# Attention with adaptive layer norm: key block 6 of the second query half goes from TensorE's sums product to GpSimd's running sums

## What is computed

```
mod = (silu(c) @ wmod).reshape(B, 6, 1, -1)            # sa, ca, ga, sb, cb, gb
h   = layernorm(x) * (1 + ca) + sa
q, k, v = h @ Wq, h @ Wk, h @ Wv                       # 32 query heads, 8 key heads, width 32; q, k rotated
att   = where(causal, q @ k.T / sqrt(32), -inf)        # four query heads share one key head
probs = softmax(att)
x = x + ga * ((probs @ v) @ Wo)
h = layernorm(x) * (1 + cb) + sb
x = x + gb * (h @ W.T + bias + lora(h))
```

## Time and profile before

| | |
|---|---|
| time, median of 3 runs (lowest to highest) | 2407.32 us (2406.97 to 2408.16) |
| profiled execution: its time | 2411.02 us |
| profiled execution: span, first to last instruction | 2409.2 us |
| busy over the span: PE / DVE / ACT / POOL | 2349.1 / 1764.7 / 1023.2 / 1577.9 us |
| GpSimd adds (L1101): number, busy | 434 (14 a group, groups 0 to 30), 921.1 us |

### The profile page before, as it was taken

How to read it: one execution, slowest core, us unless ns; L and a number is a source line. 1 busy time by engine, 2 the same in 40 slices (tenths; PEclk the granted TensorE clock), 3 DMA queues, 4 the chain that set the end, 5 groups by cost and what they waited for, 6 DMA issues and landing times. The chain is left out here.

```text
span 2409.2 us, 37318 instructions
## 1 busy us (share of the span) xinstructions
PE 2349.1 (98%) x13260; PEld 1647.3 (68%) x13260; DVE 1764.7 (73%) x4224; ACT 1023.2 (42%) x1868; POOL 1577.9 (65%) x834
## 2 busy tenths in 40 slices
PE   5999999999999999999999999998999999999998
PEld 3788888888655555555555555544788888888886
DVE  4766667667999999999999999975545545555553
ACT  3433333331466666666666666775111111111111
POOL 3743334341698998999989999984654654654653
PEclk8999999999999999999999999999999999999999
DMA  6523333334355336334343345404323333333330
GB/s 239 200 88 115 121 120 118 123 110 122 92 165 154 85 88 175 83 83 134 77 103 86 86 138 124 103 19 151 110 93 104 107 94 99 111 95 96 113 89 27
DMA packets 179716, 267.22 MB, mean 111 GB/s; under 512 B 20508, under 2 KB 113884, under 8 KB 178400
## 3 DMA queue, kind: packets, MB, share of 16 engines
q1 hardware_dynamic: 179552, 265.13, 37.3%
HBM read 183.22 MB, written 80.81 MB: 110 GB/s over the span
## 5 line engine op out<-in xcount | busy, mean ns | idle before, releaser
L1101 POOL TENSOR_TENSOR p_sum<-p_sum,p_ring 128x768 f32<-128x768 f32 (+1 forms) x434 | 919.4, 2154 | 67.9 <-PE ctx_ps L1162 44.6
L995 ACT ACTIVATE p_ring<-scores 128x512 f32<-128x512 f32 (+1 forms) x896 | 444.3, 575 | 299.4 <-DVE scores L1049 224.3
L290 DVE CUSTOM_DVE_ANT_0 scores_q<-scores_q,mask_row 128x512 f32<-128x512 f32 x977 | 458.6, 514 | 33.8 <-PE scores_q L277 33.5
L277 PE MATMUL scores_q<-k_stack,q_stack 96*128 96x512 f32 (+1 forms) x1473 | 437.7, 372 | 6.6 <-DVE neg_max L290 6.0
L277 PEld LDWEIGHTS scores_q<-k_stack,q_stack 96*128 96x128 f32 x1473 | 252.9, 190 | 211.0 <-DVE neg_max L294 96.9
L1141 PE MATMUL scores<-q_stack,k_stack 98*128 98x512 f32 (+1 forms) x1216 | 371.7, 395 | 1.7 <-DVE neg_max L290 0.9
L646 POOL TENSOR_TENSOR roped_hilo<-roped_hilo 128x512 fp32r<-128x512 f32 x80 | 105.3, 1316 | 337.2 <-ACT roped_hilo L489 337.2
L294 DVE TENSOR_REDUCE neg_max<-scores_q 128x1 f32<-128x512 f32 x496 | 313.0, 684 | 3.6 <-PE scores_q L277 1.5
L695 PE MATMUL proj_ps<-h_hi,w_hi 128*128 128x512 f32 x752 | 297.8, 396 | 0.7 <-POOL w_lo L635 0.7
L695 PE MATMUL proj_ps<-h_hi,w_lo 128*128 128x512 f32 x752 | 293.6, 390 | 0.0
L695 PE MATMUL proj_ps<-h_lo,w_hi 128*128 128x512 f32 x752 | 293.2, 390 | 0.0
(11 more groups left out here) (169 smaller groups left out, 3657.2 us busy)
## 6 DMA issues: line engine op xcount, KB each, us to landing
q_stack<-qk_t SPq DMA_DIRECT2D x96, 512.0 KB, 6.9
qk_t<-roped_hilo SPq DMA_DIRECT2D x80, 512.0 KB, 2.8
x_in<-in_L_attn_resid SPq DMA_DIRECT2D x32, 512.0 KB, 6.3
ctx_t<-ctx_raw SPq DMA_DIRECT2D x64, 256.0 KB, 7.5
prefetched<-in_L_wmod SPq DMA_DIRECT2D x4, 4096.0 KB, 14.7
prefetched<-ctx_t SPq DMA_DIRECT2D x31, 512.0 KB, 4.1
prefetched<-inv_t SPq DMA_DIRECT2D x124, 128.0 KB, 5.4
k_stack<-qk_t SPq DMA_DIRECT2D x96, 128.0 KB, 8.7
```

The lines of the kernel that those rows point to most:

```text
L277: last = nc.tensor.matmul(dst[:, a, :], qs[0:MHI, h, i * P:(i + 1) * P], ks[0:MHI, lo:lo + w], start=True, stop=True)
L290: last = nc.vector.tensor_tensor_reduce(src[:, a, :], src[:, a, :], sh.maskW[:, HALF - w:HALF], -1.0, LARGE, ALU.add, ALU.min, neg[:, a, :])
L995: nc.scalar.activation(p[:, a * per:(a + 1) * per, :], src[:, a * per:(a + 1) * per, :], ACT.Exp, scale=SM_SCALE).then_inc(s_ex.sem, 1)
L1101: nc.gpsimd.tensor_tensor(a, a, probs(n, u), ALU.add).then_inc(s_ap.sem, 1)
```

## The change

Key block 6 of half 1 (tick 18) leaves `TAIL`: GpSimd gets an add for it, and the sums product no longer takes it out of the ring. `NP` rises from 14 to 15 adds a group and `POOL_DONE[1]` with it. The hand-written order is laid anew: the sums product of half 1 of the group before moves from behind tick 5 to behind tick 13, the maxima are spread over the ticks otherwise, quads 5, 6 and 7 come together behind tick 15, and `INV_AT` is moved by four ticks.

```diff
-TAIL_FROM = {0: 4, 1: 6}
+TAIL_FROM = {0: 4, 1: 7}
...
-INV_AT = (9, 12, 15)
+INV_AT = (13, 16, 19)
...
 AFTER = [
     [],
-    maxima(1, 10, 11, 12) + quads(-1, 10, 11) + maxima(1, 13, 14),
+    maxima(1, 10, 11, 12) + quads(-1, 10, 11) + maxima(1, 13),
...
-    maxima(1, 18, 19) + quads(0, 1) + sums_of(-1, 1) + maxima(1, 20),
-    maxima(1, 21, 22),
-    maxima(1, 23) + quads(0, 2, 3) + maxima(1, 24, 25),
...
+    maxima(1, 18) + quads(0, 1) + maxima(1, 19),
+    maxima(1, 20) + quads(0, 2),
+    maxima(1, 21, 22) + quads(0, 3),
...
+    maxima(1, 34) + sums_of(-1, 1) + maxima(1, 35, 36),
     [],
-    maxima(2, 1) + quads(0, 6, 7) + turned(1) + maxima(2, 2),
+    maxima(1, 37) + maxima(2, 0, 1) + quads(0, 5, 6, 7) + turned(1) + maxima(2, 2),
```

More of the change, by code:

```diff
@@ L113 @@
     [],
-    maxima(1, 10, 11, 12) + quads(-1, 10, 11) + maxima(1, 13, 14),
-    [],
-    maxima(1, 15) + quads(0, 0) + maxima(1, 16, 17),
-    [],
-    maxima(1, 18, 19) + quads(0, 1) + sums_of(-1, 1) + maxima(1, 20),
-    maxima(1, 21, 22),
-    maxima(1, 23) + quads(0, 2, 3) + maxima(1, 24, 25),
[L121 to L127, removed]
-    maxima(2, 1) + quads(0, 6, 7) + turned(1) + maxima(2, 2),
+    maxima(1, 10, 11, 12) + quads(-1, 10, 11) + maxima(1, 13),
+    maxima(1, 14),
+    maxima(1, 15) + quads(0, 0),
+    maxima(1, 16, 17),
+    maxima(1, 18) + quads(0, 1) + maxima(1, 19),
+    maxima(1, 20) + quads(0, 2),
+    maxima(1, 21, 22) + quads(0, 3),
+    maxima(1, 23, 24, 25) + quads(0, 4) + maxima(1, 26),
+    maxima(1, 27),
+    maxima(1, 28, 29, 30),
+    maxima(1, 31),
+    maxima(1, 32, 33),
+    maxima(1, 34) + sums_of(-1, 1) + maxima(1, 35, 36),
+    [],
+    maxima(1, 37) + maxima(2, 0, 1) + quads(0, 5, 6, 7) + turned(1) + maxima(2, 2),
     maxima(2, 3),
```

## The result

The changed kernel took **2439.64 us** (median of 4 runs, 2437.72 to 2442.7), the kernel before 2407.74 in the same comparison: ratio 1.0127, 95% interval 1.0115 to 1.014; the two medians are 31.9 us apart. Forecast were 2434.7 us and +27.4, in a range of 2426 to 2450. The profiled execution has a span of 2440.9 us, against 2409.2.

A forecast was written before the change was run, and what follows sets the result against it. TensorE, coupled with VectorE, bounds the attention; GpSimd would take over. Its longer chain and later last add give +26.9, then -0.6, -0.6 and +1.7 clock: +27.4 on 2407.32, so 2434.7 us, range 2426 to 2450.

The forecast's parts named there:

- GpSimd becomes the bound by an unbroken chain: Ordinary attention groups: GpSimd's gapless adds take 32.54 us a group against 31.14 before; given chance 0.81.
- waits at half-switches and modulation places: GpSimd's 1.13 us wait for values each group, and its waits around four modulation parts, were to vanish.
- Price of the add 2.56 us: GpSimd's one new add a group: 2.39 us plus a 0.17 us gap; at least 2.34.
- floor 29.98: GpSimd's adds of one group before the change, without the wait for values: 29.98 us, read in groups 28 and 29.
- The lead of TensorE, some 11 us: TensorE may run some 11 us ahead of GpSimd before the sums product holds it, swallowing GpSimd's irregular waits.
- TensorE's saving of 0.62 us: Four 256-column products a group leave TensorE: worth at most 0.62 us, only where TensorE sets the pace.
- its pace 30.5: TensorE alone would need about 30.5 us a group after the change.
- idle 2 us a group: TensorE would stand idle about 2 us a group waiting for GpSimd, at no cost.
- rival 3: The add hides and TensorE's saving shows: groups 0.62 us shorter, -19 us, 2388 us; chance 0.03.
- The end of the attention: +1.7 for the clock, -0.6, -0.6: Around the last sums product: +1.7 us low clock, -0.6 for the shorter product, -0.6 for values moved ahead.
- The clock term: After TensorE's estimated 15 us stop in group 31, one low-clock window loses 1.7 us; bounds nothing to 3.4.
- Rival 2: TensorE's clock falls in every group at the new 2 us stop: +42 us, 2477 us; chance 0.04.

The follow-up runs named there:

- e2: Kernel before, old order, with GpSimd's fifteenth add (tick 18) added; 2450.9 us, ratio 1.0177.
- e1: Changed kernel's new order without the fifteenth add, key block 6 of half 1 again summed by TensorE; 2427.7 us, ratio 1.0081.
- e3: Changed kernel with neither add nor sums product for key block 6 of half 1 in groups 0 to 30; 2413.4 us, ratio 1.0018.
- e4: Changed kernel, but GpSimd adds the smaller key block 7 (tick 19) and TensorE keeps key block 6; 2428.3 us, ratio 1.0088.
- e5: Kernel before with the fifteenth add and only the half 1 sums product and finished-sums loading moved, to tick 13; 2440.2 us, ratio 1.0135.
- e9: Changed kernel, but in group 30 alone TensorE sums ticks 16, 17 and 18 instead of GpSimd; 2441.7 us, ratio 1.0141.
- e10: As e1 (new spread, 14 adds), but the half 1 sums product back behind tick 5; 2444.4 us, ratio 1.014.
- e8: As e5, but GpSimd adds tick 18 only in every third group (ten groups), TensorE sums it otherwise; 2444.9 us, ratio 1.0148.
- e6: Kernel before, 14 adds, only the half 1 sums product and finished-sums loading moved to tick 13; 2439.6 us, ratio 1.0137.
- e12: Kernel before, 14 adds, half 1 sums product moved one tick, between the two maxima behind tick 6; 2438.4 us, ratio 1.0112.

## Why the prediction was right

- *GpSimd becomes the bound by an unbroken chain.* Shown. 32.51 us a group, forecast 32.54; waits at half-switches and modulation places gone. The add is the cause and not the order: e2 has the old order and the same 32.5, e1 and e3 have the new order without the add and groups of 31.5 and 31.1. The times don't add up: the order alone costs 17.9 us (e1), the add alone 41.1 (e2), both together 31.9. The forecast could leave the order's price out only because the chain of adds is longer still.
- *Price of the add 2.56 us, floor 29.98.* Shown. (The floor was read in groups 28 and 29 "where TensorE has less to do". The number is right, the reason isn't: TensorE's turns were 31.3 to 31.9 apart there. GpSimd had been put back by its two other operations, at 1476.62 and 1526.57, and worked off a backlog until 1595.) The price is shown also by the smaller add of e4 (31.35, forecast 31.43). GpSimd's chain as a whole grew by 25.0 us from first add to last, 27.4 forecast: 1.4 less over the thirty groups (32.51 and not 32.54 each, and rounding), 0.8 less in group 0, where the half-switch came 8.2 us after the first add and not 8.9, 0.2 less in group 30.
- *The lead of TensorE, some 11 us, and what it swallows.* Shown, by e2 against e5 and the changed kernel: 2451 and 2440. The lead fills up slowly, 1.4 us a group less what the modulation parts take: until about group 20 the turns are 31.08 apart, then 32.3 and more. Of the first 21 sums products of half 1 none waited more than 0.34 us for GpSimd; the 22nd, at 1351.8, was the first to wait over 1 us.
- *TensorE's saving of 0.62 us, its pace 30.5, idle 2 us a group.* Wrong in size. The saving is 0.42 (e1 and e3), and the new order costs 0.37, so its pace is 31.08. I took the order as free. Nor does TensorE stand 2 us in each group: it waits over 1 us at six sums products, 1.27 to 2.76 us each, and 11.92 at the last. It changed nothing in the result, because this term lay beside the chain and not in it; it is why rival 3, 2388 us, was never within reach, by e3.
- *The end of the attention: +1.7 for the clock, -0.6, -0.6.* Undersized. From the last L1194 to the linear half it took 27.4 us before and 31.3 after, +3.9 where +0.5 was forecast. The clock term, 1.7 us, was too small. Windows of the changed kernel show why, behind two waits from inside the attention:

```profile
1516.36 1.93 PE L1194 MATMUL scores_q<-p_sum,ones_v 128*32 128x512 f32 x8 [2.76 <-POOL p_sum L1101]
1583.59 1.28 PE L1194 MATMUL scores_q<-p_sum,ones_v 128*32 128x512 f32 x8 [2.45 <-POOL p_sum L1101]
...
1516.00:1520.00 4.00, 3.64 (x20) 1.75 (x21) 0.51 (x1) 0.58 (x1) 3.86 (x3) 0.57 0.00 0
...
1640.00:1644.00 4.00, 0.00 (x0) 0.00 (x0) 0.00 (x0) 0.00 (x0) 4.00 (x3) 0.50 0.00 0
1644.00:1648.00 4.00, 0.00 (x0) 0.00 (x0) 0.00 (x0) 0.00 (x0) 3.83 (x2) 0.50 0.00 0
1648.00:1652.00 4.00, 3.71 (x26) 1.35 (x30) 0.00 (x0) 0.75 (x2) 0.23 (x1) 0.50 0.00 0
1652.00:1656.00 4.00, 3.88 (x37) 1.65 (x30) 0.00 (x0) 2.49 (x5) 0.00 (x0) 0.93 0.18 68
1656.00:1660.00 4.00, 3.78 (x10) 1.52 (x8) 0.00 (x0) 3.83 (x8) 0.00 (x0) 0.93 0.00 2
1660.00:1664.00 4.00, 3.82 (x12) 1.30 (x16) 0.86 (x2) 3.63 (x8) 0.00 (x0) 0.50 0.02 6
1664.00:1668.00 4.00, 4.00 (x32) 1.07 (x28) 0.00 (x0) 0.10 (x1) 0.00 (x0) 0.72 0.00 0
```

  The clock is at its lower level, 1.2 GHz, from 2.6 us into the stop and for the first 4 us of work, and a second time from 1659 to 1666, in a stretch where TensorE waits for ScalarE between products. I had counted one window; the kernel before has 1.00 in every window from 1620 to 1648. Summed as in the earlier trace rows, these windows behind 1648 lose 4 x (0.50 + 0.07 + 0.07 + 0.50 + 0.28) = 5.7 us of clock, part of it beside ScalarE's work. In e5, with a stop of 12.03 us, the clock didn't fall a second time (1.00 from 1654.9 to the linear half), and from the last L1194 to the linear half it took 1.4 us less than here. Its windows there:

```profile
1648.00:1652.00 4.00, 3.49 (x22) 1.15 (x26) 0.00 (x0) 0.58 (x1) 0.45 (x1) 0.50 0.00 0
1652.00:1656.00 4.00, 4.00 (x43) 2.01 (x46) 0.00 (x0) 2.13 (x4) 0.00 (x0) 0.64 0.05 19
```

  By that the second fall is worth some 1.4 us and the rest of the miss belongs to the first, which lasted 4 to 6 us into the work; the pieces around the last product differ between the two kernels, so the split is rough. e9 halves the stop, and the clock falls twice nevertheless.

- *Rival 2, the clock inside the attention.* The mean clock over all adds was 0.99. The clock fell twice, at 1516.0 and at 1584.3, for 3.4 us each (one such window, at 1516, heads the windows above), both times at the longest waits at L1194, 2.76 and 2.45 us; at the four waits of 1.27 to 1.36 us it stayed at 1.00. There GpSimd set the pace and had no gap over 0.17 us, so it cost nothing. The Trainium skill, TensorE: Matmul & The Clock Gate, in its section on HAM oscillation, has the lower clock return after the pause of every iteration. In the changed kernel it returned at two of thirty.
- *The start.* GpSimd's first add came at 635.89 instead of 632.51 us. In the profiles of the ten other variants it lies between 629.9 and 634.5, whatever the edit, so I put most of these 3.4 us to the execution. With it the span adds up: 3.4 - 2.4 (chain) - 0.3 (last wait) + 3.4 (end) + 0.2 (linear half) = 4.3 us, by which the span of 2440.9 passed the 2436.6 forecast. The chain came out too long in the forecast and the end too short, and these two misses cancel in part, which is luck. The medians, 2439.6 measured and 2434.7 forecast, are 4.9 us apart; the other executions have no trace, so whether the late start is theirs too isn't known.

No version faster than the kernel before was found. What stays open is what holds the groups of e1 and e10, when a short stop lowers the clock, and why TensorE found nothing to run for a while in the linear half of e8 and e9.

## What to carry to other kernels

When two engines are within a few per cent of each other in a stage, work handed from one to the other must be priced as a chain on the receiver, dependency gaps included; here one timeline of GpSimd gave the new group length to 0.03 us, and the giver's saving never entered. A wait on the slower engine should stand as late as its buffers allow: the lead that this gives absorbed every irregular stretch, 11 us of the total in e2 against the changed kernel. But moving even one product in a hand-laid order can cost more than shortening it gives, here most likely by starving a third engine: time the moved order alone before crediting it with nothing.

## What was not expected of the hardware

In e8 and e9, whose attention is coded with lists for each group, TensorE lost time in two tiles of the linear half, whose code is unchanged. The chain of waits of e9 in that stretch:

```profile
1879.97 7.25 PE pf L1620 x32
1887.22 4.16 issue
1891.38 1.96 PE pt L1610 x8
1893.34 11.49 PE po L1573 x48
```

For 4.16 us in the middle of the tiles TensorE waited for nothing that the profile shows ("issue"). The clock was then at 1.2 GHz from 1891.0 to 1894.4, and the two groups of products behind the gap took 1.96 and 11.49 us, a tile earlier 0.87 and 10.89: 1.7 us more. With a second gap of 1.67 us at 2074.38 that makes 7.5 us, all of e9's longer linear half. In e8 the two gaps are 2.89 and 1.66 us. The DMA view shows more traffic of the instruction queue in these two kernels:

```profile
q8 instruction: 108, 1.77, 0.3%
```

108 packets in e9 and 109 in e8, against 90 in the changed kernel and 92 in the kernel before, e6, e10 and e12. This suggests that instructions came late, but was not tested. A few microseconds in a part of a program that an edit doesn't touch can so come from the edit, and e9's gain was hidden by it.
